# Cross-attention and spline feed-forward: gate and up in eight classes with one stationary matrix per product

## The reference

```python
# x: (4, 512, 512), ctx: (4, 512, 256); all float32
q, k = ctx @ Wq.T + bq, ctx @ Wk.T + bk                 # 128 wide
att  = softmax(q @ k.T)                                  # (4, 512, 512)
x    = x + layernorm(x) @ att.T
h    = layernorm(x)
gate_w, up_w = spline(gate_cp), spline(up_cp)            # (2048, 512), from some 8100 control points
down_w       = spline(down_cp)                           # (512, 2048)
x    = x + (silu(h @ gate_w.T) * (h @ up_w.T)) @ down_w.T
```

## Time and profile before

| | us |
|---|---|
| median of 3 runs | 267.11 |
| lowest, highest | 267.0, 267.25 |
| span of the profiled execution | 265.8 |
| busy in it: TensorE, its weight loads | 247.6, 171.8 |
| busy in it: VectorE, ScalarE, GpSimd | 188.2, 123.6, 132.2 |

### The profile page before, as it was taken

How to read it: one execution, slowest core, us unless ns; L and a number is a source line. 1 busy time by engine, 2 the same in 40 slices (tenths; PEclk the granted TensorE clock), 3 DMA queues, 4 the chain that set the end, 5 groups by cost and what they waited for, 6 DMA issues and landing times.

```text
span 265.8 us, 4144 instructions
## 1 busy us (share of the span) xinstructions
PE 247.6 (93%) x1400; PEld 171.8 (65%) x1400; DVE 188.2 (71%) x332; ACT 123.6 (46%) x206; POOL 132.2 (50%) x138
## 2 busy tenths in 40 slices
PE   7879649999899999999999999999999999599995
PEld 2223136855475868884858788848586888286684
DVE  0598996698778776866788768667887686465533
ACT  3035542325469652336696523366965233254320
POOL 0398717186883831314939313149393131487800
PEclk9968977999999999999999999999999999889999
DMA  6999107000091000022720000227000002200004
GB/s 184 335 427 419 42 16 297 6 0 2 0 353 44 2 1 2 0 79 79 276 118 0 0 0 0 79 79 296 20 0 0 0 0 79 79 2 0 0 2 158
DMA packets 7355, 23.11 MB, mean 87 GB/s; under 512 B 1201, under 2 KB 2481, under 8 KB 5937
## 3 DMA queue, kind: packets, MB, share of 16 engines
q1 hardware_dynamic: 7344, 22.98, 23.1%
HBM read 18.78 MB, written 4.19 MB: 86 GB/s over the span
## 4 chain that ended last, share of the span: by engine, by line
PE 79%; DVE 10%; ACT 3%; DMA 2%; issue 2%; POOL 1%; SPq 1%; DVEq 0%; POOLq 0%
PE bank L1327 12%; PE bank L1330 12%; PE bank L1372 11%; PE bank L1344 6%; PE bank L1174 5%; PE bank L1279 5%; PE bank L1281 5%; PE bank L1280 5%; DVE prod L876 4%; PE bank L1379 3%; PE bank L1236 3%; PE bank L1192 3%; DMA power<-in_g_power 2%; PE bank L1294 1%; PE bank L1356 1%
## 5 line engine op out<-in xcount | busy, mean ns | idle before, releaser
L1124 POOL TENSOR_TENSOR ih<-inter,ones 128x512 fp32r<-128x512 f32 x64 | 65.0, 1042 | 21.5 <-DVE inter L964 21.4
L964 DVE TENSOR_TENSOR inter<-inter,bank 128x512 f32<-128x512 f32 x64 | 43.7, 686 | 18.1 <-ACT inter L776 14.9
L776 ACT ACTIVATE inter<-bank 128x512 f32<-128x512 f32 x64 | 37.9, 598 | 23.7 <-PE bank L1330 23.6
L1372 PEld LDWEIGHTS bank<-d_r,ih 128*128 128x128 f32 x256 | 31.0, 191 | 7.8 <-issue 5.9
L1372 PE MATMUL bank<-d_r,ih 128*128 128x192 f32 x256 | 32.2, 276 | 0.0
L747 ACT ACTIVATE qk<-bank,nmr,rstd 128x512 f32<-128x512 f32 x16 | 12.5, 780 | 36.7 <-PE bank L1281 19.7
L1327 PE MATMUL bank<-xh,gate_r 128*128 128x512 f32 x64 | 27.6, 431 | 1.5 <-DVE zg L956 1.5
L1111 POOL TENSOR_TENSOR xres<-x,ones 128x2048 f32<-128x2048 f32 x4 | 14.4, 3602 | 24.0 <-DMA out<-xres 23.7
L1330 PE MATMUL bank<-zg,up_v 102*128 102x512 f32 x64 | 25.9, 404 | 0.0
L1327 PE MATMUL bank<-xh,up_r 128*128 128x512 f32 x64 | 25.7, 402 | 0.0
L1330 PE MATMUL bank<-zg,gate_v 102*128 102x512 f32 x64 | 25.6, 400 | 0.0
(11 more groups left out here) (108 smaller groups left out, 454.1 us busy)
## 6 DMA issues: line engine op xcount, KB each, us to landing
x<-in_x SPq DMA_DIRECT2D x4, 1024.0 KB, 5.1
xT<-in_xT SPq DMA_DIRECT2D x4, 1024.0 KB, 7.1
out<-xres SPq DMA_DIRECT2D x16, 256.0 KB, 2.1
ctxT<-in_ctxT SPq DMA_DIRECT2D x4, 512.0 KB, 7.6
rd<-in_d_r SPq DMA_DIRECT2D x2, 768.0 KB, 6.1
knots<-in_d_knot SPq DMA_DIRECT2D x1, 1280.0 KB, 11.7
...
```

The costliest lines, as they stand in the source:

```text
L776: nc.scalar.activation(inter[:, m], gbank[m % 2][:], ACT.Silu).then_inc(s["silu_done"], 1)
L964: V.tensor_tensor(inter[:, m], inter[:, m], ubank[m % 2][:], ALU.mult).then_inc(s["mult_done"], 1)
L1124: G.tensor_tensor(ih[:, m], inter[:, m], ones[:, 0].broadcast_to([P, TOK]), ALU.mult).then_inc(s["ih_done"], 1)
L1372: mm(in_blocks(obank[t][:], i // CLS), ih[:, m, t * P:(t + 1) * P], d_r[:, i], start=m == 0, stop=False, skip_group_check=True)
```

## The change

Gate and up get eight classes of 64 columns (`G_CLS`). The nodes are spaced evenly, and the functions of a class are 20 (five periods by four powers), in three precision parts 60 rows. Residual (64 rows) and coefficients (60 rows, padded to 64) now stand in one stationary matrix `gw`; the moving matrix `mv` holds the class's 64 columns and its 60 function rows. One matmul of 128 rows per product takes the place of two. The function values depend on the class now: `replicate` is four turns, by the matrices `turns` (made by `turn_matrix` on the host), each one pair of matmuls into a full bank, one copy on ScalarE and two operations of 64 rows on VectorE. Turns 0 and 1 stand around q and k, turn 2 after tile 3 and turn 3 after tile 7. `cast_t` copies each transposed tile in halves: ScalarE one of full height and one of 64 rows, VectorE one of 64 rows.

Down has four classes of cells in place of eight, in two phases; the residual of a tile touches 36 columns in each of eight groups, 288 in all, in place of 48 in four.

`low_x`, the low part of x, is GpSimd's; on its queue it stands behind the 16 copies to `ih`. The preparation has another order: gate and up residuals are eight steps of one multiply and two adds of 64 rows by 256 columns, down 16 steps of one multiply of 2 x 288 columns and one add of 288; node weights are four steps. The inputs for the residuals of down are loaded at the start and no longer behind a wait.

The diff, cut to its core:

```diff
-G_NODES = 4 * CLS + 1
-G_FN = 2 * G_NODES
+HALF = 64
+QUAD = 32
+G_CLS = 2 * CLS
+SPAN = PERIOD / G_CLS
+OFFSET = -2.88
+PERIODS = 4
+TERMS = 4
+G_FN = (PERIODS + 1) * TERMS
 G_K = 3 * G_FN
+G_COLS = INTER // G_CLS
...
+PHASES = 2
+D_CELLS = 32
+D_CLS = 2 * PHASES
+D_SLACK = 2.6
+D_OUTER = 47.0
+GRP = HID // HALF
+BLK = 36
+D_FIRST = (0, HALF - BLK)
+STRIP = GRP * BLK
+RES = 4 * CLS + MT
...
                 st.split_windows(t)
             st.keep_warm(2)
             st.powers(0)
-            for r in range(2):
+            for r in range(4):
+                st.spread(r)
                 st.residual(r)
             for t in range(3, 7):
                 st.keep_warm(t)
-            for r in range(2):
+            st.powers(1)
+            for r in range(4, 8):
                 st.spread(r)
-            st.residual(2)
-            st.keep_warm(7)
-            st.residual(3)
-            for t in range(8, 10):
+                st.residual(r)
+            for t in range(7, 10):
                 st.keep_warm(t)
-            st.spread(2)
-            st.powers(1)
-            st.node_weights(0)
-            st.spread(3)
-            for r in range(4, 6):
-                st.residual(r)
+            for u in range(2):
+                st.node_weights(u)
             st.stats(0)
-            st.spread(4)
-            st.node_weights(1)
-            st.spread(5)
+            st.split_x(0)
+            st.qk(0, 0)
             st.node_weights(2)
-            st.split_x(0)
-            st.qk(0)
+            st.qk(0, 1)
             st.node_weights(3)
             st.jump_inputs()
-            st.node_weights(4)
-            for t in range(2):
-                st.softmax(0, t)
-            st.residual(6)
+            st.low_x(0)
             for t in range(2):
                 st.energy(0, t)
-            st.spread(6)
-            st.node_weights(5)
-            st.softmax(0, 2)
-            st.spread(7)
-            st.softmax(0, 3)
+                st.softmax(0, t)
+            for t in range(2, 4):
+                st.energy(0, t)
+                st.softmax(0, t)
             st.jumps()
             st.scale(0)
-            st.residual(7)
-            st.energy(0, 2)
             st.mean_shift(0)
...
             for t in range(2):
                 st.add_xm(0, t)
-            st.residual(8)
+            for r in range(8, 10):
+                st.residual(r)
             st.add_xm(0, 2)
-            for r in range(9, 11):
+            for r in range(10, 12):
                 st.residual(r)
-            st.spread(8)
+            for r in range(8, 10):
+                st.spread(r)
             st.add_xm(0, 3)
-            for r in range(11, 13):
+            for r in range(12, 18):
                 st.residual(r)
             for t in range(2):
                 st.prob_t(0, t)
-            st.spread(9)
             st.keep_warm(10)
             for t in range(2, 4):
                 st.prob_t(0, t)
             for t in range(11, 13):
                 st.keep_warm(t)
             st.cast_t(0, 0)
-            st.residual(13)
+            for r in range(18, 20):
+                st.residual(r)
             st.cast_t(0, 1)
             st.keep_warm(13)
             for t in range(3):
                 st.xm(0, t)
-            st.residual(14)
+            for r in range(10, 12):
+                st.spread(r)
             st.xm(0, 3)
-            st.residual(15)
-            st.spread(10)
+            for r in range(20, 24):
+                st.residual(r)
+            for r in range(12, 14):
+                st.spread(r)
             st.keep_warm(14)
-            st.spread(11)
+            for r in range(14, 16):
+                st.spread(r)
             for t in range(15, 20):
                 st.keep_warm(t)
-            st.spread(12)
+            for r in range(16, 18):
+                st.spread(r)
             st.norm_t(0, 0)
             st.cast_t(0, 2)
             st.norm_t(0, 1)
-            st.spread(13)
+            for r in range(18, 20):
+                st.spread(r)
             st.norm_t(0, 2)
             st.cast_t(0, 3)
             st.norm_t(0, 3)
-            for r in range(14, 16):
+            for r in range(20, 24):
                 st.spread(r)
...
         def ffn(st, b, a=None):
 
             st.project(b)
             if a is not None:
-                st.qk(a)
-            else:
-                st.replicate(b)
-            for m in range(4):
-                st.activate(b, m)
+                st.qk(a, 0)
+            for t in range(2):
+                st.replicate(b, t)
+            if a is not None:
+                st.qk(a, 1)
             for m in range(4):
                 st.gate_up(b, m)
-            for m in range(4):
+                st.activate(b, m)
                 st.round_inter(b, m)
+            st.replicate(b, 2)
             for m in range(4, 8):
+                st.gate_up(b, m)
                 st.activate(b, m)
-                st.gate_up(b, m)
                 st.round_inter(b, m)
+            st.replicate(b, 3)
...
                 st.split_x(a)
+                st.low_x(a)
             st.down(b, 0, range(0, 12))
...
                 def cast_t(b, t):
                     act.wait_ge(s["xn2T_mm"], NT * b + t + 1)
-                    nc.scalar.activation(xn2T[:, t], abank[t % 2][:], ACT.Copy).then_inc(s["xn2t_copied"], 1)
+                    nc.scalar.activation(xn2T[:, t], abank[t % 2][:], ACT.Copy).then_inc(s["xn2t_first"], 1)
+                    nc.scalar.activation(mv[half(1), 2 * t + 1], abank[t % 2][half(1)], ACT.Copy).then_inc(s["xn2t_copied"], 1)
...
+                def replicate(b, t):
+                    act.wait_ge(s["zg_mm"], CLS * b + t + 1)
+                    if t >= 2:
+                        act.wait_ge(s["zg_done"], 2 * (CLS * b + t - 1))
+                    nc.scalar.activation(zs[:, t % 2], zbank[t % 2][:], ACT.Copy).then_inc(s["zg_hi"], 1)
 
...
-                        dve.wait_ge(s["r_in"], 32)
-                    if r >= 2:
-                        dve.wait_ge(s["res_done"], r - 1)
+                    if r >= 4:
+                        dve.wait_ge(s["res_done"], sums(before(r)))
+                    if r < 2 * CLS:
+                        if r == 0:
+                            dve.wait_ge(s["r_in"], 16)
+                        V.tensor_tensor(prod[:, r % 4], bank[r % 4][:], g_r[:, r % CLS], ALU.mult).then_inc(s["res_mul"], 1)
+                        return
                     if r == 2 * CLS:
-                        dve.wait_ge(s["rd_in"], 32)
-                    n = r % CLS if r < 2 * CLS else r - 2 * CLS
-                    for k, part in enumerate((r2g, r3g) if r < 2 * CLS else (rd2, rd3)):
-                        width = HID if r < 2 * CLS else 2 * STRIP
...
                 def cast_t(b, t):
-                    dve.wait_ge(s["xn2t_copied"], NT * b + t + 1)
-                    V.tensor_copy(xn2r[:, t], xn2T[:, t]).then_inc(s["xn2r_done"], 1)
+                    dve.wait_ge(s["xn2t_first"], NT * b + t + 1)
+                    V.tensor_copy(mv[half(0), 2 * t], xn2T[half(0), t]).then_inc(s["xn2r_done"], 1)
...
-                def replicate(b):
-                    dve.wait_ge(s["zg_hi"], b + 1)
-                    V.scalar_tensor_tensor(zg[:], zg[:].bitcast(f32), g_low[:, 0:1], zgbank[0:G_K, :], ALU.mult, ALU.add).then_inc(s["zg_done"], 1)
+                def replicate(b, t):
+                    dve.wait_ge(s["zg_hi"], CLS * b + t + 1)
+                    for n in range(2):
+                        part = half(1 - n)
+                        V.scalar_tensor_tensor(mv[part, 2 * t + n], zs[part, t % 2].bitcast(f32), z_low[part], zbank[t % 2][part], ALU.mult, ALU.add).then_inc(s["zg_done"], 1)
...
+                    pool.wait_ge(s["res_mul"], r + 1)
...
-                    G.tensor_tensor(dst, prod2[:, r % 2, 0, 0:width], prod2[:, r % 2, 1, 0:width], ALU.add).then_inc(s["res_done"], 1)
+                        if r % CLS == 0:
+                            pool.wait_ge(s["power_done"], r // CLS + 1)
+                        for n in range(2):
+                            part = half(n)
+                            G.tensor_tensor(gw[part, r // CLS, 2 * (r % CLS) + n], prod[part, r % 4, 0:G_COLS], prod[part, r % 4, G_COLS:HID], ALU.add).then_inc(s["res_done"], 1)
+                        return
+                    if r == 2 * CLS:
+                        pool.wait_ge(s["node_mm"], CLS)
+                    k = 2 * (r % 2)
+                    G.tensor_tensor(d_r[:, r - 2 * CLS], prod[:, k, 0:STRIP], prod[:, k + 1, 0:STRIP], ALU.add).then_inc(s["res_done"], 1)
 
                 def prob_t(b, t):
...
+                def low_x(b):
+                    pool.wait_ge(s["xh_done"], b + 1)
+                    G.tensor_tensor(xl[:], xT[:], xh[:].bitcast(f32), ALU.subtract).then_inc(s["xsplit_done"], 1)
...
-                        pe.wait_ge(s["res_mul"], 2 * (r - 1))
+                    if r >= 4:
```

(44 more changed lines are left out.)

541 lines of the change are left out of this document (278 added, 263 removed).

## The result

The changed kernel takes 310.5 us against 267.1 in the same session, 1.162 times as long (95% interval 1.156 to 1.168). The forecast was 288 with 272 to 300: the direction was right, the amount was not, and the time lies above the range. The profiled execution spans 308.7 us, 42.9 more than the one of before (265.8).

The account below looks back on a forecast made before the run. TensorE, busy 93% before, was to wait for other engines, chiefly VectorE's queue. 265.8 + 5.1 preparation + 12.5 passes + 3.0 clock + 0.6 last batch = 287.0, plus 1.3 from span to median, rounded to 288; range 272 to 300.

Parts of the forecast that it names:

- Front half of a pass: VectorE's queue before the softmax's maxima: seven more 64-row operations, +4.6 us; multiply 8 at 21.6 instead of 19.1.
- Subtract: Low part of x on GpSimd: takes 4.5 us, ends at 34.9, and stalls TensorE 1.2 before the value matmuls.
- Wide matmuls: Down residual on TensorE, 288 columns for 192: 0.134 us per matmul, +1.5 us per batch.
- Casts: ScalarE's copies of the transposed norm, 0.49 apart: project starts 4.7 after the first transpose for 3.35, +1.35 per pass.
- Clock: TensorE's clock falls while other engines lead in a pass's first half: 1.0 us per pass, 3.0 in all.
- Preparation: Before the loop: head +1.4, tail +4.6, less 0.9 in the first pass; +5.1 us (0 to +8).
- Last batch: Gate and up at GpSimd's pace, turns delay, down starts earlier, wide matmuls cost 1.2: +0.6 us (-1 to +2).
- (a): Rival: TensorE stays the bound, kernel faster at 252; decided by multiply 8 no later than some 17; chance 0.11.
- (b): Rival: clock stays low through the gate and up stages, 4.7 per pass for 1.0, 299; chance 0.12.
- (c): Rival: the subtract on GpSimd is no wait and the clock holds, 281.7; chance 0.25.
- (d): Rival: the preparation comes out even, with (c) beside it, 276; chance 0.08.

Follow-up runs that it names:

- e7: Changed kernel without turns 2 and 3 of each batch; tiles 8 to 15 use the functions of the first two turns: 295.5 us (292.0 to 298.6).
- e2: Changed kernel with the low part of x subtracted on VectorE in all batches: 304.4 us, ratio 1.135 to the kernel before.
- e11: Kernel before with a second ScalarE copy, of partitions 64 to 127, behind each transposed tile's copy: 275.8 us, ratio 1.029.
- e9: Changed kernel with GpSimd's four products of the down taps held until VectorE has scaled the probabilities: 305.8 us, ratio 1.144.
- e1: Changed kernel with TensorE's fillers 15 to 19 ahead of down spreads 14 and 15 instead of behind them: 307.8 us, ratio 1.151.
- e10: Changed kernel with three repairs: products held until probabilities are scaled, fillers ahead of the spreads, low x on VectorE everywhere: 297.7 us, ratio 1.116.

## Why the prediction was right in direction and wrong in size

**Front half of a pass: right, a little short.** Third pass, forecast and measured: first multiply 7.7 and 8.2, multiply 4 at 11.9 and 12.7, maxima 16.2 and 17.2, multiply 8 at 21.6 and 22.6, down 27.2 and 28.5. The mechanism was the one named (VectorE's queue), and e7 agrees with it. Mis-sized was the low part's pitch: 0.66 was taken from the earlier trace rows; four in 3.08 with a last one of 0.75 are 0.78 apart, 0.9 us over the eight.

**Subtract: right.** 4.5 to 4.6 us, released by GpSimd as said; TensorE stands idle for 0.7 (1.2 forecast). The value matmuls start at 36.0 for 34.9, all of it from the later front. e2 takes it away: 1.0 a pass.

**Wide matmuls: right.** 12 in 1.80 with starts 0.13 apart; the row's estimate of 0.134 and its 1.5 us per batch hold. Between down and the value matmuls e2's pass has 0.8 more than before, from there to the transposes 0.7 more. The 0.8 a batch that the prediction worked out from the Trainium skill was too low.

**Casts: mechanism right, size wrong.** 1.35 forecast, 2.27 measured; e11 gives 2.2 alone. The term that was mis-sized is the pitch of 0.49, read from two equal copies; it is 0.61 to 0.62.

These make a full-clock pass 59.3 against 57.25 forecast. In parts over before: front 1.45 (down at 28.46 for 27.01), wide matmuls 1.6, stall for the subtract 0.8, casts 2.3, together 6.2.

**Clock: partly right, too little.** TensorE did lose the clock in passes where other engines kept it waiting, though in only two of the three, and the same gap in e2 cost nothing. Three passes lost 3.4 + 1.5 + 0 = 5.0 against 3.0. More than half stands in the first pass, where the preparation handed TensorE over at the lower level; the same four matmuls took, there and in the third pass,

```profile
86.54 3.78 PE L1235 MATMUL bank<-ctxT,wqk 128*128 128x512 f32 x4
...
209.20 1.98 PE L1235 MATMUL bank<-ctxT,wqk 128*128 128x512 f32 x4
```

**Preparation: wrong, and this is the step that failed.** 5.1 forecast (0 to 8): 6.0 at the first project, near 71, less 0.9 that the first pass was to give back. The project came at 84.7, 19.2 late: 8.5 at the transposes of the probabilities (1.4 forecast), 10.7 behind them (4.6 forecast). Two things were not in the sum at all. The prediction costed VectorE's jumps and the softmax as if they stood alone, though the new order puts GpSimd's subtract and products beside them; a row of before hinted at it, as its jump inputs on GpSimd had taken 3.20 for 1.27 beside VectorE's subtract of x. e9 gives 4.6 of the 19.2 (5.1 at the transposes of the probabilities). And it counted the steps ahead of the first transpose by VectorE's and GpSimd's pace alone, not the fifteen fillers in TensorE's queue, which now stand behind a wait: 3.4 by e1. With both mended, and the subtract on VectorE, the first project stands at 75.9 (e10), still 10.4 late, of which the forecast had 6.0: 4.4 at the transposes of the probabilities, 3.1 more to the first transpose of the norm, 2.9 more to the project (of which the casts 2.0 by e11: 5.63 for 3.67 from the first transpose to the project). The rest wasn't taken apart.

**Last batch: 1.3 for 0.6,** inside its bounds.

**The rivals.** (a) is out: TensorE is busy for 82%, and multiply 8 came at 22.6, far behind 17. (b) is out: all clock losses of the loop come to 5 us, not 14. (c) and (d) are out: the subtract is a wait, and the preparation isn't even. The range failed in the preparation, to which its high end allowed 8 us; the full-clock pass, at +6.2, lies just over its upper bound of 5.8. Two slips in the sums change none of this: rival (c) comes to 281.7 only from the unrounded 288.3, and the high end of 302 leaves out the 1.3 between span and median, with which it is 303.5.
